# Two edits in the attention half of a fused attention and feed-forward layer: where a block transpose writes, and when the first feed-forward loads are issued

## Chip, cores and metric

One NeuronCore of a Trainium2 chip runs the whole kernel. The metric is the device time of one launch in microseconds, as the median of several runs.

## The reference, cut to what matters

`x` is 32 blocks of 128 tokens by 512 channels in float32. For each block the layer computes

```
n  = layernorm(x)                                # per token, eps 1e-5
q  = rms_norm(n @ wq.T + bq) ; k = rms_norm(ctx @ wk.T + bk) ; v = ctx @ wv.T + bv
a  = softmax(q k^T / sqrt(32)) v                 # 16 heads of 32
x2 = x + tanh(g_xattn) * (a @ wo.T + bo)
y  = layernorm(square(relu(layernorm(x2) @ up)) @ down + (layernorm(x2) @ expert) * top2sum)
out = x2 + tanh(g_ffn) * y
```

The context is no longer than 128 tokens, so only the reference's image keys and values occur. Every product is made from three matrix multiplies on high and low parts of both operands (hi·hi, hi·lo, lo·hi), so each operand is split once into a rounded "hi" part and a "lo" remainder.

## The kernel before, in words

The kernel has two halves in one program. The first is the attention half, a software pipeline over 32 blocks. Each engine has a function `slot(s, par)`, called here **turn** s, and runs turns -1 to 30 one after another, then a drain for block 31. In turn s the engines do the score and softmax work of block s, the projections of block s + 1 (K, then Q), the probability transposes and values of block s - 1 and the output projection of block s - 2. The engines are tied by semaphores only; the order on each engine is the order written in the code. The second half, the feed-forward, runs over 8 groups of 4 blocks.

**How the normalised x gets transposed.** PE needs the normalised block with channels on partitions. The first three blocks are transposed by PE itself. From block 3 on ("dealt" blocks), the work goes round PE:

- DVE normalises block s + 2 into `xn` (`normalise`, L487).
- SP stores `xn` to `xd_scratch` in DRAM in runs of 32 channels (L273) and, when the store has landed, loads it back as `x_dealt` (L280). Between the two it issues the load of a later `xin` block (L240).
- DVE transposes 32x32 blocks from `x_dealt` to `x_turned` (`turn_blocks`, L499), near the end of turn s.
- ACT copies `x_turned` to `xnT_hi` (`hi_xT`, listed under its helper line L660) and DVE takes the difference into `xnT_lo` (`lo_xT`, listed under L473). The rows call both tiles `eight`.
- PE's Q projection of turn s + 1 waits for `xnT_lo`.

Before the change the DVE transpose reads and writes unbroken rows. The tokens of a row of `x_turned` are then not in order, and `hi_xT` and `lo_xT` put them right: through `by_blocks` they read runs of 32, and through `in_order` they access the `xnT` tiles with a step of 4 words from element to element.

**SP's queue.** SP issues nearly all transfers of this half, in code order. In turn s it loads `xres`, stores and reloads the dealt block, loads `xin` and the context `cin`, stores `x2` of block s - 2, and moves pieces of the feed-forward weights. At the end of turns 23 to 27 it also calls `ff.load_first(sp, s - 23)`, which brings the first data of the feed-forward: four blocks of `x2` (`fx<-x_scratch`, L1060), four pieces of the up weights (`fy<-in_up`, L1067), the gate weights, and gamma and beta. The four `x2` blocks are read through a view that deals the rows:

```python
def dealt_rows(a):
    return a.rearrange("(b c) n -> c b n", c=KT)      # KT = 4
```

Their first readers are `ff.stats` on DVE, one block in each of the turns 24 to 27 (L1260). The up pieces are first read by POOL's `up_sums` in turn 28, the gate weights by ACT at the end of turn 30, gamma and beta at the end of the drain.

PE's part of a turn is: scores (L346), K projection, Q projection, twelve transposes of probabilities (L368), output projection (`wo`), and then values, further transposes and the V projection. The output projection of turn s waits for DVE's `qb` (L583), which takes Q's result out of its bank. On DVE the order at the start of a turn is `vb` (L535), `lo_xT` (L473), four maxima (L505), and after sums and exponentials by ACT, `xn` (L487) and `qb` (L583).

Of the kernel before, what the change touches and what calls it, by code (L numbers as in the profile page):

```python
# [13 lines left out]
KT = D // P  # L14
# [9 lines left out]
def flamingo_layer(nc, t, out):  # L24
# [6 lines left out]
    NB = t["x"].shape[0]  # L31
    GB = D // P
# [6 lines left out]
    def at_least(eng, sem, value, apart=False):  # L39

        if isinstance(value, int) and value <= 0:
            return
        eng.wait_ge(sem, value)
        if apart and not isinstance(value, int):
            eng.sem_inc(passed[eng], 1)

    with ExitStack() as whole:
        def sem(name):  # L50
            return whole.enter_context(nc.semaphore(name))

        def sb(ctx, name, shape, dt=F32):
            return ctx.enter_context(nc.sbuf_tensor(name, shape, dt))
# [40 lines left out]
        with ExitStack() as ctx:  # L95
# [9 lines left out]
            x_dealt, x_turned = sb(ctx, "x_dealt", [P, D]), sb(ctx, "x_turned", [P, D])  # L105
# [24 lines left out]
            st_xd, ld_xd, dv_xt = sem("st_xd"), sem("ld_xd"), sem("dv_xt")  # L130
# [4 lines left out]
            dv_kb, dv_qb, dv_kf, dv_xT, dv_aT, dv_vb, dv_mx, dv_rr, dv_bs, dv_st, dv_xn, dv_p = (  # L135
                sem("dv_" + n) for n in ("kb", "qb", "kf", "xT", "aT", "vb", "mx", "rr", "bs", "st", "xn", "p"))
            ac_sk, ac_sq, ac_xT, ac_pT, ac_aT, ac_kT, ac_qT, ac_qf, ac_c, ac_e = (
                sem("ac_" + n) for n in ("sk", "sq", "xT", "pT", "aT", "kT", "qT", "qf", "c", "e"))
# [12 lines left out]
            def has(b):  # L151

                return not isinstance(b, int) or 0 <= b < NB
# [5 lines left out]
            def is_slot(b, n):  # L159
                return isinstance(b, int) and b == n  # L160
# [3 lines left out]
            def dealt(b):  # L164

                return not isinstance(b, int) or XD <= b < NB

            def dealt_count(b):
                return (b - (XD - 1)) * DMA
# [36 lines left out]

                return slice(h * HD, (h + 1) * HD)

            def by_blocks(a):

                return a[:, :].rearrange("p (c k b) -> p k c b", c=KT, k=KT)

            def in_order(a):

                return a[:, :].rearrange("p (k b c) -> p k c b", c=KT, k=KT)

            def by_strip(a):

# [13 lines left out]
            def _(sp):  # L232
# [6 lines left out]
                def load(b, par, src, dst, s):  # L239
                    sp.dma_start(dst[par][:, :], src[b]).then_inc(s[par], DMA)  # L240
# [24 lines left out]
                def slot(s, par):  # L265
                    a, n, o = s - 1, s + 1, s - 2
                    if has(a):
                        at_least(sp, dv_x2, a - 1, apart=True)
                        load(a, 1 - par, t["x"], xres, ld_r)
                    if dealt(s + 2):  # L270
                        at_least(sp, dv_xn, s + 3, apart=True)
                        there = xd_dram[par].rearrange("(i b) (c k d) -> (b c) k i d", i=HG, c=KT, k=KT)
                        sp.dma_start(there, xn[:, :].rearrange("p (k i d) -> p k i d", k=KT, i=HG)).then_inc(st_xd, DMA)  # L273
                    if has(s + 4):
                        at_least(sp, dv_xn, s + 3, apart=True)
                        load(s + 4, par, t["x"], xin, ld_x)
                    if dealt(s + 2):
                        at_least(sp, st_xd, dealt_count(s + 2), apart=True)
                        at_least(sp, dv_xt, s + 2 - XD, apart=True)
                        sp.dma_start(x_dealt[:, :], xd_dram[par]).then_inc(ld_xd, DMA)  # L280
                    if has(s + 4):
                        at_least(sp, ac_c, s + 3, apart=True)
                        at_least(sp, po_c, s + 3, apart=True)
                        load(s + 4, par, t["ctxT"], cin, ld_c)
                    if has(o):
                        at_least(sp, dv_x2, o + 1, apart=True)
                        sp.dma_start(x2_dram[o], x2[par][:, :]).then_inc(st_x2[par], DMA)
                    if ff.has_half(s - 3):
                        ff.q_store(sp, s - 3, 1 - par)
                    if ff.has_half(s - 1):  # L290
                        ff.q_load(sp, s - 1, 1 - par)
                    if is_slot(s, NB - 9):
                        for m in range(2):
                            sp.wait_ge(st_x2[m], GB // 2 * DMA)
                    if isinstance(s, int) and NB - 9 <= s < NB - 4:
                        ff.load_first(sp, s - (NB - 9))

                def drain(s, a, o):
# [12 lines left out]
                    sp.dma_start(x2_dram[s], x2[s % 2][:, :]).then_inc(st_x2[s % 2], DMA)  # L311

                run(sp, slot, before, drain)

            @block.tensor
# [155 lines left out]
            def _(dve):  # L471
                def sub(dst, a, hi):
                    return dve.tensor_tensor(dst, a, hi.bitcast(F32), ALU.subtract)  # L473
# [15 lines left out]
                def lo_xT(b):  # L489
                    at_least(dve, ac_xT, b + 1)  # L490
                    if dealt(b):
                        sub(in_order(xnT_lo), by_blocks(x_turned), in_order(xnT_hi)).then_inc(dv_xT, 1)
                    else:
                        sub(xnT_lo[:, :], BTX, xnT_hi[:, :]).then_inc(dv_xT, 1)

                def turn_blocks(b):
                    at_least(dve, ld_xd, dealt_count(b))
                    at_least(dve, ac_xT, b)
                    dve.transpose(x_turned[:, :], x_dealt[:, :]).then_inc(dv_xt, 1)  # L499

                def maxima(b, g):

# [44 lines left out]
                def slot(s, par):  # L547
# [6 lines left out]
                    if has(n):  # L554
                        lo_xT(n)
# [49 lines left out]
                    if dealt(n + 1):  # L605
                        turn_blocks(n + 1)
# [51 lines left out]
            def _(act):  # L658
                def copy(dst, src):
                    return act.activation(dst, src, ACT.Copy)  # L660

                def hi_xT(b):
                    if dealt(b):
                        at_least(act, dv_xt, b - (XD - 1))
                        at_least(act, pe_Q, b)
                        copy(in_order(xnT_hi), by_blocks(x_turned)).then_inc(ac_xT, 1)
                    else:
                        at_least(act, pe_Tx, b + 1)
                        copy(xnT_hi[:, :], BTX).then_inc(ac_xT, 1)
# [25 lines left out]
                def before():  # L695
                    row(act, bk, "bk", ld_bk)
                    row(act, tgbo, "nq", ld_n)
                    row(act, junk_q, "nk", ld_n)
                    row(act, bq, "bq", ld_bq)
                    hi_ctx(0, 0)  # L700
                    weight_hi(0, 0)
                    hi_xT(0)
                    for k in range(1, KT):
                        weight_hi(0, k)
                    for k in range(KT):
                        weight_hi(1, k)
# [29 lines left out]
                def slot(s, par):  # L736
# [44 lines left out]
                    if has(n + 1):  # L781
                        hi_xT(n + 1)
# [144 lines left out]
def feed_forward_start(nc, whole, t, x2_dram, bank, ident, tanh_g, powers, W, fx, fy, pair, eight, ring_dram, at_least, mm3):  # L927


    NB = t["x"].shape[0]  # L930
    NI = t["up"].shape[1] // D
    NE = t["gate"].shape[1] // KT
    GB = D // P
# [5 lines left out]
    def sb(name, shape, dt=F32):  # L939
        return whole.enter_context(nc.sbuf_tensor(name, shape, dt))  # L940
# [16 lines left out]
    c = [sb("c0", [P, 2, D])]  # L957
# [88 lines left out]
    def q_stored(sp):  # L1046
        for n in range(2):
            sp.wait_ge(st_q[n], (NS // 2 + 1) * 2 * DMA)
# [9 lines left out]
    def load_x(sp, g, j):  # L1058
        if static(g) and g == 0:
            sp.dma_start(xn[j], dealt_rows(x2_dram[j])).then_inc(ld_x[j], DMA)  # L1060
        else:
            sp.dma_start(xn[j], x2_dram[g * GB + j]).then_inc(ld_x[j], DMA)

    def load_piece(sp, p):
        if p >= GB:
            taken(sp, p - GB)
        sp.dma_start(stage_at(p), t["up"].rearrange("p (i n) -> p i n", i=NI)[:, p, :]).then_inc(ld_s[p % GB], DMA)  # L1067

    def load_first(sp, n):
        if n == 0:  # L1070
            q_stored(sp)
            for pos in range(GB):
                load_x(sp, 0, X_ORDER[pos])
        elif n < 3:
            for p in range(2 * n - 2, 2 * n):
                load_piece(sp, p)
        elif n == 3:
            sp.dma_start(ga_raw[:, :, :], t["gate"].rearrange("p (k n) -> p k n", k=KT)).then_inc(ld_g, DMA)
            sp.dma_start(two_ident[:, :], t["two_ident"]).then_inc(ld_g, DMA)
        else:  # L1080
            for src, dst in (("gamma", gamma), ("beta", beta)):
                sp.dma_start(dst[:, :], t[src].broadcast_to([P, D])).then_inc(ld_g, DMA)
# [861 lines left out]
```

## Time and profile before

| | |
|---|---|
| three runs, lowest, median, highest | 1365.27, 1367.46, 1367.71 us |
| profiled execution, its own time | 1364.38 us |
| its span, first to last instruction | 1362.5 us |
| mean granted TensorE clock | 0.995 of full speed |
| attention half, feed-forward half | about 0 to 563 us, then to the end |

The profile is of one execution. PE is TensorE's matrix multiplies, DVE the vector engine, ACT the scalar engine, POOL GpSimd, SP the engine that issues transfers, PEld PE's weight loads. Times of rows are microseconds from the start of the span unless marked ns. A turn is best seen from one start of the scores (L346) to the next: turn 24 starts at 416.44 us, turn 25 at 432.56, turn 26 at 452.47. SP runs ahead of PE: the end of its turn 23 lies at 415 us.

### The profile page before, as it was taken

To read this page: it belongs to the slowest core of one execution; us is meant where nothing else is said; L and a number is where in the kernel's file an instruction comes from. 1 tells how busy PE (TensorE), PEld (TensorE's weight loads), DVE (VectorE), ACT (ScalarE), POOL (GpSimd) and SP (SyncE) were. 2 spreads that over 40 slices of the span, in tenths; PEclk is the share of its full clock that TensorE was granted. 3 is DMA by queue.
4 is the path that set the end of the run, shared out by engine and by line. 5 is a ranking of instruction groups with operands and counts; after the bars stand their busy time and mean duration, and the time that the engine had idled before them with its cause. 6 is when DMAs were issued, how large, how long until landed. Compare 5 with 4: busy or idle time off the path is not lost.

```text
span 1362.5 us, 27965 instructions
## 1 busy us (share of the span) xinstructions
PE 1323.2 (97%) x9148; PEld 1127.5 (83%) x9148; DVE 922.6 (68%) x1768; ACT 624.7 (46%) x1891; POOL 542.8 (40%) x671
## 2 busy tenths in 40 slices
PE   6899999999999999999999999999999999999996
PEld 5688888888887787888888888888888888898984
DVE  5566666666665666886776775775775776776764
ACT  4788887878886877432312212223213113223210
POOL 3566666676765875542131140140140240240211
PEclk9999999999999999999999999999999999999998
DMA  6245555555544432448449459458368468377541
GB/s 234 70 125 147 147 145 139 150 155 156 142 131 134 115 96 70 164 146 219 157 148 250 139 152 251 130 156 258 124 176 246 130 173 244 117 180 221 176 142 37
DMA packets 279123, 214.37 MB, mean 157 GB/s; under 512 B 186640, under 2 KB 186768, under 8 KB 279056
## 3 DMA queue, kind: packets, MB, share of 16 engines
q1 hardware_dynamic: 246800, 154.78, 40.7%
q10 hardware_dynamic: 32256, 58.73, 13.0%
q8 instruction: 37, 0.61, 0.2%
q14 instruction: 30, 0.25, 0.1%
HBM read 163.92 MB, written 49.55 MB: 157 GB/s over the span
## 4 chain that ended last, share of the span: by engine, by line
PE 83%; issue 5%; DVE 4%; ACT 2%; DMA 1%; POOL 1%; ACTq 0%; POOLq 0%; DVEq 0%
PE bank L76 16%; PE bank L77 16%; PE bank L78 16%; PE wide L77 8%; PE wide L78 8%; PE wide L76 8%; PE bank L368 3%; PE wide L380 2%; PE bank L331 2%; PE wide L346 2%; ACT prob L687 1%; DMA xd_scratch<-xn 1%; DVE c L1344 1%; PE wide L1537 0%; PE wide L1534 0%
## 5 line engine op out<-in xcount | busy, mean ns | idle before, releaser
L1611 ACT ACTIVATE hT_hi<-c 128x512 fp32r<-128x512 f32 x128 | 80.0, 631 | 403.2 <-PE wide L78 216.0
L1843 POOL TENSOR_TENSOR pair<-pair,beta 128x512 f32<-128x512 f32 x28 | 39.2, 1398 | 450.4 <-DMA pair<-x_scratch 450.4
L687 ACT ACTIVATE prob<-wide,nmx 128x128 f32<-128x128 f32 x512 | 182.2, 403 | 72.1 <-DVE nmx L505 68.9
L77 PE MATMUL wide<-wo_lo,hT_hi 128*128 128x512 f32 x512 | 203.3, 397 | 0.0
L78 PE MATMUL wide<-wo_hi,hT_lo 128*128 128x512 f32 x512 | 201.9, 394 | 0.0
L76 PE MATMUL wide<-wo_hi,hT_hi 128*128 128x512 f32 x512 | 201.4, 393 | 0.0
L847 POOL TENSOR_TENSOR prob<-prob,rr 128x512 f32<-128x512 f32 x128 | 137.0, 1071 | 85.7 <-DVE rr L513 84.2
L1689 DVE TENSOR_TENSOR hT_lo<-c,hT_hi 128x512 fp32r<-128x512 f32 x128 | 97.8, 784 | 74.7 <-ACT hT_hi L1611 74.1
L687 ACT ACTIVATION_READ_ACCUMULATOR prob<-wide,nmx 128x1 f32 x512 | 124.0, 242 | 0.0
L78 PEld LDWEIGHTS wide<-wo_hi,hT_lo 128*128 128x128 f32 x512 | 96.1, 188 | 22.7
L76 PEld LDWEIGHTS wide<-wo_hi,hT_hi 128*128 128x128 f32 x512 | 96.2, 188 | 21.6
L77 PEld LDWEIGHTS wide<-wo_lo,hT_hi 128*128 128x128 f32 x512 | 96.1, 188 | 20.6
L76 PE MATMUL bank<-wq_hi,up_hi 128*128 128x256 f32 x384 | 108.4, 282 | 3.0 <-DVE c L1317 3.0
L77 PE MATMUL bank<-wq_lo,up_hi 128*128 128x256 f32 x384 | 107.8, 281 | 0.0
L78 PE MATMUL bank<-wq_hi,up_lo 128*128 128x256 f32 x384 | 107.7, 281 | 0.0
L1344 DVE SCALAR_TENSOR_TENSOR c<-c 128x512 f32<-128x512 f32 x128 | 83.9, 698 | 0.0
L78 PE MATMUL bank<-wv_hi,up_lo 128*128 128x256 f32 x288 | 81.2, 282 | 0.0
L77 PE MATMUL bank<-wv_lo,up_hi 128*128 128x256 f32 x288 | 80.9, 281 | 0.0
L76 PE MATMUL bank<-wv_hi,up_hi 128*128 128x256 f32 x288 | 80.8, 281 | 0.0
L505 DVE TENSOR_REDUCE nmx<-wide 128x4 f32<-128x512 f32 x128 | 79.3, 684 | 0.0
L76 PEld LDWEIGHTS bank<-wq_hi,up_hi 128*128 128x128 f32 x384 | 72.4, 189 | 3.8 <-DVE c L1317 3.8
L660 ACT ACTIVATE pT<-bank 128x512 f32<-128x512 f32 x122 | 74.8, 667 | 0.0
(229 smaller groups left out, 3590.5 us busy)
## 6 DMA issues: line engine op xcount, KB each, us to landing
wo_hi<-ring_scratch ACTq DMA_DIRECT2D x110, 256.0 KB, 3.6
wo_lo<-ring_scratch ACTq DMA_DIRECT2D x110, 256.0 KB, 4.5
wo_hi<-ring_scratch SPq DMA_DIRECT2D x46, 256.0 KB, 2.7
wo_lo<-ring_scratch SPq DMA_DIRECT2D x46, 256.0 KB, 2.9
fx<-x_scratch SPq DMA_DIRECT2D x36, 256.0 KB
xin<-in_x SPq DMA_DIRECT2D x32, 256.0 KB, 3.3
cin<-in_ctxT SPq DMA_DIRECT2D x32, 256.0 KB, 2.8
xres<-in_x SPq DMA_DIRECT2D x32, 256.0 KB, 3.9
```

The source lines that it names most:

```text
L76: eng.matmul(dst, ah, bh, start=first and k == 0, stop=False)
L77: eng.matmul(dst, ah, bl, start=False, stop=False)
L78: mm = eng.matmul(dst, al, bh, start=False, stop=last and k == n - 1)
L368: mm = pe.transpose(cols(dst, h), prob[par][:, g, h * P:(h + 1) * P], ident[:, :])
L505: dve.tensor_reduce(nmx[:, g * HG:(g + 1) * HG], bank[g].rearrange("p (h k) -> p h k", h=HG), AX.X, ALU.max, negate=True).then_inc(dv_mx, 1)
L660: return act.activation(dst, src, ACT.Copy)
L687: i = act.activation(prob[par][:, g, h * P:(h + 1) * P], cols(bank[g], h), ACT.Exp, bias=nmx[:, n:n + 1], scale=1.0, accum_out=rs[:, n:n + 1])
L847: pool.tensor_tensor(p, p, r, ALU.mult).then_inc(po_p, 1)
L1344: dve.scalar_tensor_tensor(out=cc[:, m, :], in0=cc[:, m, :], scalar=0.0, in1=cc[:, m, :], op0=ALU.max, op1=ALU.mult).then_inc(dv_h, 1)
L1611: return act.activation(dst, src, ACT.Copy)
L1689: dve.tensor_tensor(ff.hT_lo[i % 2][:, :], ff.c[i // 2 % 2][:, i % 2, :], ff.hT_hi[i % 2][:, :].bitcast(F32), ALU.subtract).then_inc(ff.dv ...
L1843: pool.tensor_tensor(res(g, j), res(g, j), ff.beta[:, :], ALU.add).then_inc(ff.po_r, 1)
```

## The change

Two things change. First, the DVE transpose of a dealt block writes `x_turned` in token order, through a view with a step of 4 words; the ACT copy and the DVE difference behind it then read and write unbroken rows, and `by_blocks` goes. Second, `load_first` is called in six turns (23 to 28) in place of five: two `x2` blocks at the end of turn 23, two in turn 24, then the up pieces in turns 25 and 26, the gate in 27, gamma and beta in 28.

```diff
             def in_order(a):
-                return a[:, :].rearrange("p (k b c) -> p k c b", c=KT, k=KT)
+                return a[:, :].rearrange("p (k b c) -> p c k b", c=KT, k=KT)
...
-                    if isinstance(s, int) and NB - 9 <= s < NB - 4:
+                    if isinstance(s, int) and NB - 9 <= s < NB - 3:
                         ff.load_first(sp, s - (NB - 9))
...
-                        sub(in_order(xnT_lo), by_blocks(x_turned), in_order(xnT_hi)).then_inc(dv_xT, 1)
+                        sub(xnT_lo[:, :], x_turned[:, :], xnT_hi[:, :]).then_inc(dv_xT, 1)
...
-                    dve.transpose(x_turned[:, :], x_dealt[:, :]).then_inc(dv_xt, 1)
+                    dve.transpose(in_order(x_turned), x_dealt[:, :].rearrange("p (c k b) -> p c k b", c=KT, k=KT)).then_inc(dv_xt, 1)
...
-                        copy(in_order(xnT_hi), by_blocks(x_turned)).then_inc(ac_xT, 1)
+                        copy(xnT_hi[:, :], x_turned[:, :]).then_inc(ac_xT, 1)
...
     def load_first(sp, n):
         if n == 0:
             q_stored(sp)
-            for pos in range(GB):
+        if n < 2:
+            for pos in range(2 * n, 2 * n + 2):
                 load_x(sp, 0, X_ORDER[pos])
-        elif n < 3:
-            for p in range(2 * n - 2, 2 * n):
+        elif n < 4:
+            for p in range(2 * n - 4, 2 * n - 2):
                 load_piece(sp, p)
-        elif n == 3:
+        elif n == 4:
```

## Rows read from the trace of the kernel before

**Rows 1.** The page's first part: busy time, share of the span, instructions.

```profile
PE 1323.2 (97%) x9148; PEld 1127.5 (83%) x9148; DVE 922.6 (68%) x1768; ACT 624.7 (46%) x1891; POOL 542.8 (40%) x671
```

**Rows 2.** Windows; columns: stretch, length, busy per engine, clock, DMA share, GB/s.

```profile
62.00:416.00 354.00, 354.00 (x2991) 291.03 (x2990) 226.62 (x418) 287.83 (x1032) 239.44 (x284) 1.00 0.51 140
...
416.44:432.56 16.12, 16.12 (x137) 13.25 (x136) 9.27 (x18) 11.63 (x45) 7.09 (x9) 1.00 0.47 137
432.56:452.47 19.91, 16.83 (x138) 13.18 (x137) 11.94 (x24) 13.68 (x47) 14.56 (x20) 1.00 0.48 125
452.47:468.59 16.12, 16.12 (x138) 13.24 (x137) 10.63 (x21) 12.81 (x47) 13.01 (x16) 1.00 0.48 131
...
517.00:533.45 16.45, 16.45 (x138) 13.26 (x137) 10.37 (x18) 13.22 (x49) 10.99 (x15) 1.00 0.10 33
```

**Rows 3.** PE's waits from 60 to 560 us: total, times, longest.

```profile
PE bank L76 <- DVE eight L473: 1.5, 1, 1.5
PE bank L76 <- DVE qb L583: 1.4, 1, 1.4
```

**Rows 4.** Timeline of DVE, a turn of usual length: start, us, instruction, idle before.

```profile
414.48 0.70 DVE L499 STREAM_TRANSPOSE x_turned<-x_dealt 128x512 f32<-128x512 f32 x1
416.55 0.69 DVE L535 TENSOR_TENSOR vb<-bank,bv 128x512 f32<-128x512 f32 x1 [1.37 <-PE bank L78]
417.16 1.08 DVE L473 TENSOR_TENSOR eight<-x_turned,eight 128x512 fp32r<-128x512 f32 x1
...
423.32 0.69 DVE L583 TENSOR_TENSOR qb<-bank,pair 128x512 f32<-128x512 f32 x1
```

**Rows 5.** Timeline of DVE at the end of turn 24.

```profile
429.99 0.69 DVE L473 TENSOR_TENSOR aT_lo<-wide,aT_hi 128x512 fp32r<-128x512 f32 x1 [0.82 <-ACT aT_hi L660]
...
435.31 0.71 DVE L499 STREAM_TRANSPOSE x_turned<-x_dealt 128x512 f32<-128x512 f32 x1 [4.63 <-DMA x_dealt<-xd_scratch]
```

**Rows 6.** Timeline of SP, turns 22 to 24: issue times of transfers.

```profile
409.68 0.33 SPq L280 DMA_DIRECT2D x_dealt<-xd_scratch  x1
...
415.77 2.59 SPq L1060 DMA_DIRECT2D fx<-x_scratch  x4
...
423.19 7.82 SPq L240 DMA_DIRECT2D xin<-in_x  x1
432.72 0.33 SPq L280 DMA_DIRECT2D x_dealt<-xd_scratch  x1
```

**Rows 7.** DMA issues, whole run, then from 410 to 440 us: median us to landing.

```profile
xd_scratch<-xn SPq DMA_DIRECT2D x29, 256.0 KB, 3.3
x_dealt<-xd_scratch SPq DMA_DIRECT2D x29, 256.0 KB, 2.6
...
xd_scratch<-xn SPq DMA_DIRECT2D x1, 256.0 KB, 10.2
```

**Rows 8.** Windows of 2 us, with four `fx` loads under way and with up pieces.

```profile
426.00:428.00 2.00, 2.00 (x14) 1.69 (x13) 0.76 (x3) 2.00 (x6) 1.55 (x3) 1.00 0.26 98
...
454.00:456.00 2.00, 2.00 (x11) 1.63 (x10) 2.00 (x5) 1.08 (x7) 2.00 (x1) 1.00 0.95 295
```

**Rows 9.** Groups by form: busy us, mean ns of one; ACT's two, then DVE's.

```profile
L660 ACT ACTIVATE eight<-x_turned 128x512 fp32r<-128x512 f32 x29 | 32.3, 1113 | 29.3 <-DVE x_turned L499 29.3
L660 ACT ACTIVATE eight<-cin 128x512 fp32r<-128x512 f32 x32 | 20.1, 629 | 5.5 <-DMA cin<-in_ctxT 5.5
...
L473 DVE TENSOR_TENSOR wo_lo<-fx,wo_hi 128x512 fp32r<-128x512 f32 x4 | 2.5, 688 | 2.8 <-ACT wo_hi L660 2.8
```

**Rows 10.** Timeline of PE, turn 24: first Q matmul, first output-projection matmul.

```profile
420.40 0.39 PE L76 MATMUL bank<-wq_hi,eight 128*128 128x512 f32 x1
...
424.35 0.48 PE L76 MATMUL bank<-wo_hi,aT_hi 128*128 128x512 f32 x1
```

**Rows 11.** Timeline of DVE, turn 30.

```profile
517.71 1.65 DVE L473 TENSOR_TENSOR eight<-x_turned,eight 128x512 fp32r<-128x512 f32 x1
```

**Rows 12.** The chain that ended last, around 530 us: start, us, what.

```profile
530.23 0.58 ACT aT_hi L660
```

More of the change, by code:

```diff
@@ L207, in strip @@
                 return slice(h * HD, (h + 1) * HD)
-            def by_blocks(a):
-                return a[:, :].rearrange("p (c k b) -> p k c b", c=KT, k=KT)
             def in_order(a):
-                return a[:, :].rearrange("p (k b c) -> p k c b", c=KT, k=KT)
+                return a[:, :].rearrange("p (k b c) -> p c k b", c=KT, k=KT)
             def by_strip(a):
```

## The prediction

> **What bounds the kernel.** I read the page's busy shares first: PE is busy 97% of the span, so time can only come from where PE isn't [rows 1]. Then I cut the attention half into windows from one start of the scores to the next. The reader is to see three things in them [rows 2]. From 62 to 416 us PE has no idle microsecond, and a turn takes 16.12 us. One turn, number 25, takes 19.91 us: 19.91 - 16.12 = 3.79 us too much. And turn 30 takes 16.45, 0.33 too much. PE's own waits say who was late in the long turn: DVE's `eight` (that is `xnT_lo`) for 1.5 us and then `qb` for 1.4 [rows 3]; the rest of the 3.79 is made of short waits and restarts.
>
> Following `eight` back: DVE sat idle 4.63 us at the end of turn 24 until `x_dealt` landed at 435.3, while it had been ready at 429.99 + 0.69 = 430.68 [rows 5]. SP issued that load only at 432.72 [rows 6]. In the turn before it was issued at 409.68; one turn of 16.12 us later would have been 425.80. Two things held it: the `xd_scratch` store took 10.2 us to land in place of 3.3 [rows 7], and the `xin` issue behind it took SP 7.82 us [rows 6]. Ahead of both stand four `fx<-x_scratch` loads, issued from 415.77 on. While they run, 0.26 of the DMA engines is busy and 98 GB/s move; with two up pieces under way it is 0.95 and 295 GB/s [rows 8]. 0.26 of 16 engines is about four: the `fx` loads seem to run on four engines, and everything with a share on those four waits behind them.
>
> That the cause is four loads of this kind, not four loads of any kind, matters: two of them stay together after the change.
>
> **The change, part by part.**
>
> *Spread loads, turn 24.* Two `fx` loads, 2 x 262 KB = 524 KB, leave the queue in front of turn 24's store. At the 98 GB/s of [rows 8] that is 5.35 us. So the store lands not at 432.72 but near 427.4 (and not before the usual 425.80), and `x_dealt` 2.6 us after its issue [rows 7], at 430.0. DVE is ready for it at 430.68: nothing is late. There is also some tolerance behind: DVE was 4.63 late and PE lost 3.79, so 0.84 is absorbed. The stall starts only if `x_dealt` lands after 430.68 + 0.84 = 431.5, so the estimate has 1.5 us to spare. The whole 3.79 comes back.
>
> *Spread loads, turn 25.* The other two are now issued at the end of SP's turn 24, one turn of 16.12 us later, where two up pieces stood. The queue is clear by then (427.4 against about 432), so this turn is as the one above: two narrow loads, then a store about 7 us later, the same 1.5 us to spare, cost nothing.
>
> The rule of the Trainium skill, page "DMA: Bandwidth & Descriptors", section "Why a DMA increments its semaphore by 16 and not by 1", is that the number of engines of such a transfer is the largest up to 16 that divides the slowest dimension of both sides; for `dealt_rows`, whose slowest dimension is 4, that gives four. The trace's 0.26 agrees. The page's table gives about 27 GiB/s for an engine; at that figure the two loads would be worth 4.5 us instead of 5.35, `x_dealt` would land at 430.8, still before 431.5, and the sum would be the same.
>
> *Moved loads, turns 25 to 28.* Up pieces go from turns 24 and 25 to 25 and 26, the gate to 27, gamma and beta to 28. Behind two pieces turn 26 ran at 16.12 [rows 2]. Their readers are in turn 28, at the end of 30 and in the drain, over a turn away. Cover: that distance; cost nothing. Without it a piece would be 16 us late.
>
> *The ACT copy.* It writes with a step of 4 words in 1113 ns; the same copy of `cin`, unbroken, takes 629 [rows 9]. So ACT wins 0.48 us in each of 29 turns. ACT isn't what PE waits for in these turns. Worth nothing by itself.
>
> *The DVE difference.* 1.08 us with a stepped source and a stepped destination [rows 4]; unbroken 0.69 [rows 9]. It saves 0.39 us, ahead of the maxima. PE has no idle time to give back in turns 3 to 24, so again nothing. But it widens two margins. Q starts at 420.40 and the difference ends at 418.24: 2.16 spare. `qb` ends at 423.32 + 0.69 = 424.01 and the output projection starts at 424.35: 0.34 spare [rows 4, 10]. The second is the narrow one; it becomes about 0.73.
>
> *The DVE transpose.* 0.70 us unbroken [rows 4]; a stepped destination is nowhere in the trace for this operation. Below, it costs what it does now, 0.70. Above, I take the worst the stepped difference ever took, 1.65 us [rows 11], 0.96 over an unbroken one, on top: 1.66. The nearest rows put a step at 0.39 (DVE, two stepped streams) to 0.48 (ACT, one) [rows 4, 9]; I take 0.70 + 0.45 = 1.15. Cover: DVE then idles 1.37 us before `vb` [rows 4]. With 1.15 the transpose ends at 415.63, ACT's copy at 416.3, both before the difference's old start at 417.16. With 1.66: 416.14 and 416.8, still before. In turns 24 to 27 `ff.stats` stands behind the transpose and the idle time is shorter, but what the transpose adds (0.45) the difference gives back (0.39) ahead of the maxima. Cost nothing in all 29 turns. Without cover, 29 x 0.45 = 13 us.
>
> The Trainium skill speaks against this step: the page "Vector Engine (DVE) Microarchitecture Reference", section 5.2, has a port at full rate only for runs of at least two adjacent words, and 2.50 ns per column for a destination that steps a few words each element. That would be an estimated 1.28 us for 512 columns plus its 0.075 per instruction, 1.36 in all; the stepped rows here point to less. The sum would be the same, since 1.36 is also under the cover.
>
> *Turn 30.* There the stepped difference took 1.65 us [rows 11], which pushed `qb` and the output projection; the turn lost 0.33 [rows 2]. The unbroken one will be shorter. Between 0 and 0.33 I take 0.2.
>
> Sum: 3.79 + 0.2 = 4.0 us less. On the profiled execution: 1364.38 - 4.0 = 1360.4. That execution stands 3.1 us under the median of the runs, so the median goes from 1367.46 to 1363.5.
>
> **The rivals.**
>
> *B: two narrow loads still hold up the store.* For it: the queue on those engines is shared, and the `xin` issue block shows that SP itself stands still. Against: 1.5 us to spare in each turn. If a pair costs 1 us in each of two turns, 2 of the 3.79 are lost: 1365.5. The engine-count rule of the DMA page named above is not touched by the change, which halves the load on the same four engines and does not widen it.
>
> *C: the stepped transpose is much dearer; the slower side.* Latest moment for the difference to start without delaying the output projection: 417.16 + 0.39 + 0.34 = 417.89. Before it come ACT's 0.63 and two handovers of about 0.05, so the transpose must end by 417.16, which is a length of 2.7 us. From there each turn loses what is over: 28 x (length - 2.7). At 2.84 us it has eaten the 4.0; at 3.0, 8.4 are lost and 1371.9 comes out. For it: no row shows this operation stepped. Against: it would have to be four times as long, and the stepped rows add at most a factor of 1.8.
>
> *D: the time comes back but is lost later.* From 530 us on, at the end of turn 30, the chain that ended last goes over from PE to ACT [rows 12], and then to DVE and POOL. If that chain hung on something not moved with PE, the gain would go: 1367.3. Against: each step of it follows from PE's values of turn 30, and with PE busy for 97% of the span [rows 1] there is little room to lose it in later.
>
> **How the numbers follow.** Forecast as described 0.74, B 0.14, C 0.06, D 0.06. Within 0.2% of 1367.46 means 1364.7 to 1370.2, about what a measurement of this kernel can tell from no change. The forecast 1363.5 is only 1.2 under this bound and the three runs spread over 2.4 us, so 0.12 of its chance falls to "same"; with B and D and a mild C, 0.26 in all. Slower needs C well past its point: 0.06. The rest, 0.68, is faster. The range: 2.5 us of spread below, B and D above: 1361.0 to 1367.3. This leaves out the strong C and the tails.
>
> **What would show it.** Right: turn 25 between two scores takes 16.12, DVE's `x_turned` waits for no DMA, SP's `xin` issue in turn 24 takes 1 to 3 us, the store lands within 5 us; DVE L499 at 1.1 to 1.2 us, ACT `eight<-x_turned` at 0.63, the difference at 0.69; turns 3 to 23 still at 16.12. Wrong: turns 25 or 26 above 16.12 with DMA before `x_turned` (B); PE waiting for `eight` or `qb` in every turn, with L499 above 2.7 us (C); a wait after 530 us that isn't there now (D).

## The result, and the profile after

The changed kernel takes 1360.45 us (median of 7 runs, 1359.63 to 1363.63); the kernel before took 1365.89 beside it (7 runs, 1365.13 to 1367.71; the median of the first three had been 1367.46). The ratio is 0.9961, with a 95% interval of 0.995 to 0.9973: 5.3 us less, by the interval 3.7 to 6.8. The direction was forecast and the forecast ratio, 1363.5 / 1367.46 = 0.9971, lies in the interval. The time itself lies 0.55 us under the lower end of my range, and 3.05 under the forecast. The spans of the two profiled executions, 1362.5 and 1358.7 us, differ by only 3.8 us.

Three windows of the profile after: turns 24, 25 and 30, from scores to scores. The columns are the stretch, its length, the busy time of PE, PEld, DVE, ACT and POOL with the number of instructions in brackets, the clock, the DMA share and GB/s. They answer to [rows 2].

```profile
416.18:432.30 16.12, 16.12 (x138) 13.24 (x137) 10.72 (x21) 12.33 (x46) 9.29 (x13) 1.00 0.47 125
432.30:448.42 16.12, 16.12 (x138) 13.24 (x137) 10.72 (x21) 12.33 (x46) 12.38 (x15) 1.00 0.51 131
512.89:529.01 16.12, 16.12 (x137) 13.24 (x136) 9.63 (x18) 13.20 (x48) 11.07 (x15) 1.00 0.11 34
```

Turn 25 fell from 19.91 to 16.12 and turn 30 from 16.45 to 16.12; every turn from 2 to 30 is now 16.11 to 16.13. The waits of PE for `eight` and `qb` of [rows 3] are gone.

The timeline of SP after, with the lines that answer to [rows 6]:

```profile
415.50 1.36 SPq L1056 DMA_DIRECT2D fx<-x_scratch  x2
...
422.52 2.44 SPq L236 DMA_DIRECT2D xin<-in_x  x1
426.73 0.33 SPq L276 DMA_DIRECT2D x_dealt<-xd_scratch  x1
...
438.64 2.71 SPq L236 DMA_DIRECT2D xin<-in_x  x1
443.12 0.33 SPq L276 DMA_DIRECT2D x_dealt<-xd_scratch  x1
```

The `xin` issue holds SP 2.4 and 2.7 us in two turns in place of 7.82 in one, and `x_dealt` is issued 6.0 us earlier than before (5.7 us, if both are counted from the scores of their turn 24, 416.18 and 416.44). The timeline of DVE after, one usual turn and then the end of turn 24 (idle time in brackets), beside [rows 4, 5]:

```profile
414.21 1.08 DVE L495 STREAM_TRANSPOSE x_turned<-x_dealt 128x512 f32<-128x512 f32 x1
416.28 0.69 DVE L531 TENSOR_TENSOR vb<-bank,bv 128x512 f32<-128x512 f32 x1 [0.99 <-PE bank L78]
416.89 0.68 DVE L469 TENSOR_TENSOR eight<-x_turned,eight 128x512 fp32r<-128x512 f32 x1
...
430.33 1.08 DVE L495 STREAM_TRANSPOSE x_turned<-x_dealt 128x512 f32<-128x512 f32 x1
```

The transpose of turn 24 waits for nothing; it follows `aT_lo` at once. It takes 1.08 us instead of 0.70, the idle time before `vb` shrinks from 1.37 to 0.99 by just that, and the difference takes 0.68 instead of 1.08. All instances of the three operations (min/median/max in ns); the one long difference, 1004 ns, is that of turn 30, where it took 1.65 us before [rows 11]:

```profile
L495 DVE STREAM_TRANSPOSE x_turned<-x_dealt x29: 1077/1084/1085, 59.6 to 510.9; 128x512 f32<-128x512 f32 x29
L656 ACT ACTIVATE eight<-x_turned x29: 631/631/634, 60.7 to 512.0; 128x512 fp32r<-128x512 f32 x29
L469 DVE TENSOR_TENSOR eight<-x_turned,eight x29: 681/681/1004, 62.3 to 513.6; 128x512 fp32r<-128x512 f32 x29
```

A third, smaller gain shows only when both profiles are read at the same place after turn 30. This is the timeline of DVE before, then after; the operation is the lo part of the first up weights, which runs beside POOL's `x_sums` (four subtractions over `x2` blocks, `tsum<-fx`). Both stand 1.39 us before the last scores of PE (533.45 and 529.01).

```profile
532.06 2.02 DVE L1220 TENSOR_TENSOR wk_lo<-fy,wk_hi 128x512 fp32r<-128x512 f32 x2
534.00 1.21 DVE L1220 TENSOR_TENSOR wk_lo<-c,wk_hi 128x1024 fp32r<-128x1024 f32 x1
```

```profile
527.62 1.70 DVE L1217 TENSOR_TENSOR wk_lo<-fy,wk_hi 128x512 fp32r<-128x512 f32 x2 [0.33 <-ACT wk_hi L1204]
529.24 1.21 DVE L1217 TENSOR_TENSOR wk_lo<-c,wk_hi 128x1024 fp32r<-128x1024 f32 x1
```

The pair takes 1.70 us instead of 2.02, and DVE goes on 0.32 us sooner against PE. POOL's part is 0.3 us further ahead against PE: the first of the four `x_sums` operations starts 3.24 us before those scores, and 2.93 before the change. So the two share less time. By the profile the gain is 3.79 (turn 25) + 0.38 (turns 29 and 30: 16.17 + 16.45 less 2 x 16.12) + 0.32 = 4.5 us. The last term is counted at its place only. It is still there, at 0.37 us, after the first of the eight groups of the feed-forward. From the second group on, the profiles differ by more than that, and none shows that it reaches the end.

### The profile page after: what moved, and what is told of

Same layout as the page of the kernel before. It is cut to its first block, busy times and chain, and to the rows that moved or that the text cites. A ratio compares the mean times of both kernels' runs of the same rounds, so it can differ in the third digit from the quotient of the medians.

```text
span 1358.7 us, 27965 instructions
## 1 busy us (share of the span) xinstructions
PE 1321.8 (97%) x9148; PEld 1127.2 (83%) x9148; DVE 928.9 (68%) x1768; ACT 615.9 (45%) x1891; POOL 531.9 (39%) x671
## 4 chain that ended last, share of the span: by engine, by line
PE 75%; issue 11%; DVE 6%; POOL 2%; ACT 1%; DMA 0%; ACTq 0%; DVEq 0%; POOLq 0%
PE bank L76 15%; PE bank L77 15%; PE bank L78 15%; PE wide L77 6%; PE wide L76 6%; PE wide L78 6%; PE bank L364 4%; PE wide L342 2%; PE wide L376 2%; PE bank L327 2%; DVE c L1341 1%; POOL yrstd L1833 1%; DVE yst L1712 1%; POOL yvar L1831 1%; ACT prob L683 0%
```

## The experiments

Eight more runs were made, each against the kernel before; one of them is the changed kernel again.

### The loads alone

```diff
 (load_first and its turns as in the change; transpose, copy and difference as before)
```

> Only the spread of the first feed-forward loads; the transpose as before. My theory: the 3.79 us of turn 25 are wholly the loads' doing, so turn 25 takes 16.12 us between two scores, turn 30 keeps its 16.45 and the total falls by 3.8 us (ratio 0.9972). Rival (the lighter copy and difference give part of the 5.4 us measured): turn 25 stays above 16.12 or the total falls by clearly less than 3 us.

Ratio 0.9967 (0.9953 to 0.9981), 4.5 us less. Windows of its turns 25 and 30:

```profile
433.94:450.06 16.12, 16.12 (x138) 13.24 (x137) 10.65 (x21) 12.75 (x46) 12.94 (x15) 1.00 0.49 136
514.59:531.02 16.43, 16.42 (x138) 13.25 (x137) 10.36 (x18) 13.23 (x49) 10.96 (x15) 1.00 0.10 33
```

Turn 25 is whole, turn 30 is as before, as expected. The 3.79 us are the loads'. Turns 25 and 30 give 3.8 of the 4.5 us; the rest is in no turn.

### The transpose alone

```diff
-                    if isinstance(s, int) and NB - 9 <= s < NB - 3:
+                    if isinstance(s, int) and NB - 9 <= s < NB - 4:
 (load_first as before; transpose, copy and difference as in the change)
```

> Only the stepped transpose with the unbroken copy and difference; all four x2 loads at the end of turn 23. My theory: worth 0.3 to 0.4 us, from turn 30 (16.45 to 16.12). Turn 25 stays within 0.3 of 19.9, since what the transpose loses after the late landing (0.38) the copy and the difference win back (0.48 and 0.40) and 0.5 is hidden by the statistics between. Ratio 0.9997. Rival (the transpose edit carries the surplus over my forecast): 1.4 us or more, ratio 0.999 or less.

Ratio 0.9995 (0.9986 to 1.0005). Windows of turns 25 and 30:

```profile
435.63:455.42 19.79, 16.83 (x138) 13.18 (x137) 12.02 (x24) 12.80 (x47) 14.31 (x19) 1.00 0.48 127
519.90:536.02 16.12, 16.12 (x138) 13.24 (x137) 9.64 (x18) 13.20 (x48) 11.06 (x15) 1.00 0.10 34
```

By the turns it is worth 0.12 + 0.38 us, and the 0.3 after turn 30: from PE's last scores to DVE's first subtraction `c<-c` with a bank (L1338 before) it is 24.65 us here and 24.62 in the changed kernel, 24.94 before and 25.01 with the loads alone. So 0.8 us, which the timing can't tell from nothing. The profile shows no surplus of 1.4 in this edit; the timing alone does not exclude one, as its interval reaches down to 0.9986, which is 1.9 us.

### Four loads, but not narrow

```diff
-            sp.dma_start(xn[j], dealt_rows(x2_dram[j])).then_inc(ld_x[j], DMA)
+            sp.dma_start(xn[j], x2_dram[j]).then_inc(ld_x[j], DMA)
```

This is the kernel before with one view changed. It leaves out the dealing of the rows, so the first group of the feed-forward gets its tokens in another order and the output isn't the reference's; bytes, number and place of the loads are the same.

> The kernel before with its four x2 loads at one place, but read in natural row order, so that the slowest dimension is 128 and not 4; group 0 of the feed-forward then has its tokens in another order than the reference. Same bytes, same number of loads. My theory (the loads are narrow, on about four DMA engines): the DMA share right behind them rises from 0.26 to above 0.8, the 1 MB is through in some 4 to 5 us, the xin issue takes 1 to 2 us and turn 25 takes 16.12: 3.8 us less in all. Rival (1 MB of any shape ahead of the store is too much): the xin issue stays above 5 us and turn 25 above 18.

Ratio 0.9976 (0.9965 to 0.9987), 3.3 us less. A window of 2 us behind the four loads, the timeline of SP, and the first scores of turns 25 and 26 on PE:

```profile
418.00:420.00 2.00, 2.00 (x10) 1.62 (x10) 2.00 (x4) 0.88 (x5) 0.00 (x0) 1.00 0.98 310
```

```profile
416.03 1.86 SPq L1060 DMA_DIRECT2D fx<-x_scratch  x4
...
423.38 1.79 SPq L240 DMA_DIRECT2D xin<-in_x  x1
426.89 0.33 SPq L280 DMA_DIRECT2D x_dealt<-xd_scratch  x1
```

```profile
432.81 1.17 PE L346 MATMUL wide<-kT,qT 32*128 32x128 f32 x32
...
448.93 1.17 PE L346 MATMUL wide<-kT,qT 32*128 32x128 f32 x32
```

The DMA share is 0.98 against 0.26 in [rows 8] (and 0.23 in the same window, 418 to 420 us, of the kernel before), SP is held 1.79 us and not 7.82, and turn 25 takes 16.12. The same megabyte at the same place costs nothing. It was the width.

### Three narrow loads and one

```diff
-            for pos in range(2 * n, 2 * n + 2):
+            for pos in (range(3) if n == 0 else range(3, 4)):
```

> The changed kernel with three x2 loads at the end of turn 23 and one in turn 24. My theory (each narrow load adds 262 KB at 98 GB/s, 2.7 us, to the store's landing; lateness is absorbed up to about 431.3): x_dealt is issued at about 429.4 and lands at 432.0, DVE waits 1.5 us for it, turn 25 takes 16.5 to 17.2 us, the whole 0.4 to 1 us more than the changed kernel; the xin issue takes about 5 us. Rival (a threshold: the queue stalls with four and not with three): turn 25 takes 16.12.

Ratio 0.9962 (0.9947 to 0.9977), which can't be told from the changed kernel. The profile can tell; window of turn 25, and the timelines of SP and DVE in front of it:

```profile
432.56:449.91 17.35, 16.42 (x137) 13.26 (x136) 11.99 (x24) 12.77 (x47) 12.10 (x15) 1.00 0.44 110
```

```profile
422.79 5.77 SPq L236 DMA_DIRECT2D xin<-in_x  x1
430.26 0.33 SPq L276 DMA_DIRECT2D x_dealt<-xd_scratch  x1
```

```profile
432.89 1.10 DVE L495 STREAM_TRANSPOSE x_turned<-x_dealt 128x512 f32<-128x512 f32 x1 [2.21 <-DMA x_dealt<-xd_scratch]
```

`x_dealt` is issued at 426.73, 430.26 and 432.72 with two, three and four narrow loads, less for the fourth than for the third. It is 2.21 us late with three, and turn 25 loses 1.23. So 0.98 is absorbed (I had 0.84), and there is no threshold between three loads and four. The landing was 0.9 us later than I had worked out, and the loss a little above the 1 us I expected at most.

### The transpose twice and three times

```diff
+            spare = [sb(ctx, f"spare{n}", [P, D]) for n in range(1)]   # range(2) for three times
...
+                    for a in spare:
+                        dve.transpose(in_order(a), x_dealt[:, :].rearrange("p (c k b) -> p c k b", c=KT, k=KT))
```

> The changed kernel with a second stepped DVE transpose of the same block in front of the real one, into a spare tile: a length of about 2.1 us in place of 1.08 in each of 29 turns. My theory (cover up to a length of 2.7 us): turns 3 to 23 stay at 16.12 and the time is that of the changed kernel within 1 us. Rival (the cover is only DVE's idle 0.99 us in front of vb, so anything over it costs): 0.1 us and more per turn, 3 us and more in all.

Ratio 0.9973 (0.9963 to 0.9983). Windows of a usual turn and of turn 27, in which the statistics stand behind the transpose:

```profile
384.13:400.25 16.12, 16.12 (x137) 13.25 (x136) 10.97 (x21) 12.87 (x47) 10.48 (x13) 1.00 0.45 131
...
464.79:481.15 16.36, 16.36 (x138) 13.26 (x137) 11.33 (x23) 12.19 (x46) 12.12 (x15) 1.00 0.47 126
```

The pair takes 1.98 us, 0.90 more than the single one, and a usual turn doesn't notice. This alone doesn't refute the rival, since DVE had idled 0.99 us there and the addition just fits into that. The turns with `ff.stats` behind the transpose do: in the changed kernel DVE idles only 0.20 to 0.30 us there, so the addition goes over it by 0.6 us and more. Turn 25 loses nothing all the same, and turns 26, 27 and 28 lose 0.06, 0.24 and 0.22. The loss goes with how late in its turn the difference (`eight<-x_turned,eight`) starts. These are its starts in turns 25 and 27:

```profile
433.72 0.68 DVE L470 TENSOR_TENSOR eight<-x_turned,eight 128x512 fp32r<-128x512 f32 x1
...
466.37 0.68 DVE L470 TENSOR_TENSOR eight<-x_turned,eight 128x512 fp32r<-128x512 f32 x1
```

With the scores of these turns at 432.49 and 464.79, it starts 1.23 and 1.58 us into the turn. The limit that I had worked out, 417.89, lies 1.45 us into turn 24. In turn 27 `qb` ends at 472.78 us and the output projection starts at 472.84, so `qb` is what it is held by, as forecast.

> The changed kernel with two extra stepped transposes into spare tiles: about 3.1 us in each of 29 turns. My theory: the point of 2.7 us is passed, the difference starts about 1.1 us late, 0.7 of it is absorbed in front of qb, so a turn takes 16.4 to 16.6 us and the time is 8 to 13 us above the changed kernel, with PE waiting for qb at the output projection. Rival (no such point, it stays hidden): turns at 16.12.

Ratio 1.0135 (1.012 to 1.015), some 24 us above the changed kernel, 19 of them in the turns. Another 4 lie behind the last scores (833.9 us to the end of the span instead of 829.7), and no run says why. A window, PE's waits from 80 to 500 us, and the timeline of DVE:

```profile
262.78:279.60 16.82, 16.38 (x137) 13.25 (x136) 12.37 (x22) 12.71 (x47) 10.21 (x13) 1.00 0.50 142
```

```profile
PE bank L76 <- DVE qb L582: 9.8, 25, 0.8
```

```profile
252.64 1.20 DVE L484 TENSOR_SCALAR xn<-xin,mv,rstd 128x512 f32<-128x512 f32 x1 [0.20 <-issue]
...
261.11 2.00 DVE L497 STREAM_TRANSPOSE spare<-x_dealt 128x512 f32<-128x512 f32 x2
262.96 1.07 DVE L498 STREAM_TRANSPOSE x_turned<-x_dealt 128x512 f32<-128x512 f32 x1
...
264.73 0.69 DVE L470 TENSOR_TENSOR eight<-x_turned,eight 128x512 fp32r<-128x512 f32 x1 [0.18 <-ACT eight L659]
```

The place is the forecast one, `qb` before the output projection. The price is not: three take 2.92 us (261.11 to 264.03), and a usual turn loses 0.5 to 0.7 where I had 0.3 to 0.5; turns 25 to 28 lose 1.0 to 1.1. `xn`, between the maxima and `qb`, takes 1.20 us here and 0.55 in a usual turn of the changed kernel. That fits with the excess, but no run separates it. The limit itself held: the difference starts 1.95 us into this turn, 0.50 behind the limit of 1.45, and the turn loses 0.70. With the turns of the run before this gives a row: starts at 1.23, 1.44, 1.57, 1.58 and 1.95 us lose 0, 0.06, 0.22, 0.24 and 0.70. So the loss begins at about 1.4 us. As a length of the transpose the limit is looser, between 1.98 and 2.92 us, since the transposes here also start 0.29 us nearer to the scores than in [rows 4] (1.67 in place of 1.96 ahead of them).

### The changed kernel again

> The changed kernel itself, once more against the kernel before. By turns its gain is 3.79 us in turn 25 and 0.38 in turns 29 and 30, 4.2 in all (ratio 0.9969); the 5.4 of the first comparison hold 1.2 more. My theory: the surplus is the spread of the executions, of the time before the first scores and of the feed-forward half, which differ by over 1 us between profiles of one kernel; the ratio then falls on either side of 0.9969 and its interval holds it. Rival (a gain outside the turns): the ratio is 0.9961 or less again and its interval stays under 0.9969.

Ratio 0.996 (0.9946 to 0.9975). All turns from 2 on are 16.11 or 16.12, so the profile repeats. The interval holds 0.9969, yet the middle fell on 0.996 again: neither side of this expectation is fully met. With the 0.32 us found after turn 30 the profile's gain is 4.5 (0.9967), and both intervals hold it. The times are 1362.26 us for the changed kernel (5 runs) and 1367.24 for the kernel before (9 runs).

### Wide stores at the end

The profile after shows the same narrowness at a place that nothing covers. Windows of the last microseconds of the changed kernel; the last DVE result ends at 1350.46, the span at 1358.7:

```profile
1350.00:1352.00 2.00, 0.00 (x0) 0.00 (x0) 0.46 (x1) 0.00 (x0) 0.00 (x0) 0.50 0.28 88
1352.00:1354.00 2.00, 0.00 (x0) 0.00 (x0) 0.00 (x0) 0.00 (x0) 0.00 (x0) 0.50 0.23 75
1354.00:1356.00 2.00, 0.00 (x0) 0.00 (x0) 0.00 (x0) 0.00 (x0) 0.00 (x0) 0.50 0.26 101
```

```diff
+    def strip_out(eng, g, j, c):
+        rows = out[g * GB + j].rearrange("(b c) n -> c b n", c=KT)[c]
+        eng.dma_start(rows, ff.y[j][c * 32:(c + 1) * 32, :]).then_inc(ff.st_o[j], DMA)
...
+            if is_last(g):                      # SP: strips 0 and 1; ACT, after its group: strips 2 and 3
+                for c in range(KT // 2):
+                    strip_out(sp, g, j, c)
+                return
```

> The changed kernel with the stores of the last four output blocks cut into their four strips of 32 rows, two issued by SP and two by ACT, so that the slowest dimension is 32 and not 4. In the changed kernel these stores run at a DMA share of 0.26 and the span goes on for 8.2 us after the last DVE result. My theory (narrow transfers, as the x2 loads): the share rises to 0.6 or more, the span ends 3.5 to 5 us after the last result, and the time is 3 to 5 us below the changed kernel, at about 0.9935 of the kernel before. Rival (the tail is the fixed time of a store and its completion, not width): 7 us or more after the last result, no gain.

Time 1356.85 us (5 runs), ratio 0.9924 (0.9909 to 0.9939): 4.9 us below the changed kernel as timed in the same comparison (0.996), and faster than both. Its last result ends at 1352.17:

```profile
1352.00:1354.00 2.00, 0.00 (x0) 0.00 (x0) 0.17 (x1) 0.00 (x0) 0.00 (x0) 0.50 0.82 228
1354.00:1355.10 1.10, 0.00 (x0) 0.00 (x0) 0.00 (x0) 0.00 (x0) 0.00 (x0) 0.50 0.04 13
```

The share is 0.82 and the span ends 2.9 us after the last result in place of 8.2. It was not the fixed time of a store. The strips keep the dealt order of the rows, so that order is not what makes a transfer slow. The run also lets ACT issue half of the strips; what this alone is worth was not tried.

## Why the prediction was right, and where it was off

- **The stall of turn 25 and its cause: right.** The loads alone bring back all 3.79 us; four loads of full width in one place do too. The narrowness, not the amount, held the store. One reading of mine was loose: beside waits of 3.1 us, the rest of the 3.79 is time in which PE counts as busy (16.83 us in turn 25 against 16.12, [rows 2]), not further waits.
- **Two narrow loads per turn fit under the cover: right.** `x_dealt` was issued at 426.73 where I had worked out 427.4, which is 0.4 us sooner when both are counted from the scores. Three would have cost 1.23 us (run), so the spare time I gave for two was of the right size.
- **The transpose costs 1.15 us, hidden: right.** It takes 1.08 and a usual turn stays at 16.12. Even 1.98 us is hidden there (run). My step from the nearest rows (0.45) was just above the measured one (0.38). The estimate from the Trainium skill ("Vector Engine (DVE) Microarchitecture Reference", section 5.2), 1.36 us, was above the measured 1.08; the page's 2.50 ns per column is for a destination that steps 24 words, and it has no row for 4.
- **Lighter copy and difference are worth nothing in turns 3 to 24: right.** 631 and 681 ns, no gain.
- **Turn 30: the term was mis-sized.** I took 0.2 of 0.33; it was all of the 0.33, and turn 29, which I had at nothing, gave another 0.05. The difference of turn 30 took 1.00 us in place of 1.65.
- **The drain: a term was missing.** I wrote that the time after turn 30 only follows PE. But POOL moved 0.3 us ahead, and 0.32 us of DVE's slowdown beside it went. With the transpose doubled POOL is 0.19 us ahead and the pair of `wk_lo` takes 1.83 us, between 1.70 and 2.02, as it should if POOL's place is the cause. That was the inverse of rival D.
- **The step that failed: from the sum to the time and its range.** The sum of 4.0 us was too small, and the range under it too narrow. Of the 3.05 us between forecast and result, 0.5 is the terms above: 0.18 for turns 29 and 30 and 0.32 for the time after them, which I had put at nothing. Another 1.57 is the level. I went from 1367.46, while the kernel before had 1365.89 beside the changed one. 1367.46 was not a wrong figure for this kernel: in the later comparisons it had 1367.52 (25 runs), 1367.14 (14) and 1367.24 (9). Beside the first result both kernels ran faster, and when the changed kernel was run again it took 1362.26 us, inside my range. The "2.5 us of spread below" allowed for scatter of single runs, not for a whole comparison that lies 1.6 us lower together with a sum that is short. The last 1.0 us is a surplus of the timing over the profile's 4.5.
- **The chances don't add up.** B at 1365.5 and D at 1367.3 both lie within 0.2% of 1367.46. With the 0.12 of the forecast that makes 0.32 for "same" even without a mild C, and not 0.26; faster should have had 0.62.

What the surplus is stays open. It may be scatter. The same account (what the turns and the time after turn 30 gave in the profile, against the timing) can be made for seven comparisons. The timing is over the profile's gain by 0.8 and 1.0 us for the changed kernel, by 0.7 for the loads alone and by 1.9 for three loads and one. It is under it by 0.1 for the transpose alone and for the transpose twice, and by 0.5 for the four plain loads. So it is over in four of the five comparisons with the loads spread, and not in the fifth. The intervals, 1.3 to 2.1 us to either side, neither show nor exclude a gain of the spread outside the turns. The profiles have none: from the last scores to the end of the span it is 829.7 to 831.2 us with the loads spread, and 829.1, 830.1 and 831.9 with them in one place. For the changed kernel it is 829.7 and 829.9 against 829.1 before, which is why the spans differ by 3.8 us and not by 4.5. Ahead of the turns the profiles scatter as well: the first scores start at 28.7 to 31.8 us, and turn 1 takes 20.4 to 21.2.

## What to carry to other kernels

Look at the DMA share, not only at the bytes, behind a transfer: here a share of a quarter with the queue full meant that the view's outer dimension was 4, and what was queued behind waited, SP's next issues included. Two narrow loads in a turn cost nothing, four in front of a round trip cost 3.79 us, and narrow stores at the very end some 5. Where an engine works ahead of the one that bounds the kernel, as DVE and ACT do here, taking cost off it paid only at the few turns where its slack ran out, and most of those could be found beforehand as the turns that weren't of the usual length. The slack is best stated as the latest start of an operation within its turn: the idle time in front of it was too small a measure.

## What the runs showed of the hardware that I had not expected

- A DVE 32x32 block transpose of 128x512 float32 takes 0.70 us unbroken and 1.08 with a destination step of 4 words; the subtraction took 0.69 and 1.08 with two stepped streams. So one stepped stream added about as much (0.38 us) to the one operation as two did (0.39) to the other.
- ACT's copy with a stepped destination takes 1113 ns, unbroken 631.
- A two-operand DVE subtraction beside POOL's subtractions is slower: two of them took 2.02 us, 1.83 with POOL 0.19 us further ahead, and 1.70 with POOL 0.3 us further ahead.
- The Trainium skill's rule on the number of engines ("DMA: Bandwidth & Descriptors", section "Why a DMA increments its semaphore by 16 and not by 1") is that a transfer runs on the largest number of engines up to 16 that divides the slowest dimension of both sides. The shares here agree: 0.26 with an outer dimension of 4, 0.98 with 128, and 0.82 with strips of 32 rows.
